# Scores computed twice in a fused attention and feed-forward kernel: once for the row maxima, once with the keys on partitions

## What is computed

```python
def _L0_xattn_ref(query, key, value, attn_mask, q_w, q_b, k_w, k_b, v_w, v_b, o_w, o_b):
    Q = proj(query, q_w, q_b)
    K = proj(key, k_w, k_b)
    V = proj(value, v_w, v_b)
    scores = jnp.einsum('bhqd,bhkd->bhqk', Q, K) / jnp.sqrt(jnp.float32(hd))
    scores = jnp.where(attn_mask, jnp.float32(-1000000000.0), scores)
    attn = jax.nn.softmax(scores, axis=-1)
    ctx = jnp.einsum('bhqk,bhkd->bhqd', attn, V)
    ctx = ctx.transpose(0, 2, 1, 3).reshape(B, S, D)
    out = jnp.einsum('bsd,ed->bse', ctx, o_w) + o_b
    return out
...
x = x + jnp.tanh(g_xattn[0]) * _L0_xattn_ref(_layernorm(x, axis=-1), ctx_1024, ctx_1024, ...)
x = x + jnp.tanh(g_ffn[0]) * _L0_ffn_ref(_layernorm(x, axis=-1), ...)
```

## Time and profile before

| | |
|---|---|
| runs | 1276.35 us median (1274.07, 1276.35, 1281.88) |
| span of the profiled execution | 1275.5 us, from first to last instruction; its own time is not listed beside it, and the span lies within the runs |
| TensorE matmul | 1184.9 us busy, 93% of the span, 7424 instructions |
| VectorE | 956.5 us, 75% |
| ScalarE | 763.2 us, 60% |
| GpSimd | 253.7 us, 20% |
| mean granted clock of TensorE | 0.977 of full |
| chain that ended last | TensorE 65%, VectorE 12%, issue 12%, GpSimd 6% |

### The profile page before, as it was taken

How to read it: one execution, slowest core, us unless ns; L and a number is a source line. 1 busy time by engine, 2 the same in 40 slices (tenths; PEclk the granted TensorE clock), 3 DMA queues, 4 the chain that set the end, 5 groups by cost and what they waited for, 6 DMA issues and landing times.

```text
span 1275.5 us, 25860 instructions
## 1 busy us (share of the span) xinstructions
PE 1184.9 (93%) x7424; PEld 933.5 (73%) x7424; DVE 956.5 (75%) x2011; ACT 763.2 (60%) x1632; POOL 253.7 (20%) x427
## 2 busy tenths in 40 slices
PE   3999899999999989999999999987999999999997
PEld 3777676777767767777676777765878878878886
DVE  5778688688778867868877887879677677777763
ACT  4678677678768867867866886774432433343332
POOL 1030030030012003003002100025433443343441
PEclk9999999999999989999998999987999999999999
DMA  6433332253243343233224332461111211211200
GB/s 216 113 96 80 100 108 61 70 143 79 64 125 89 79 98 91 76 99 106 75 59 134 82 83 59 115 196 52 51 50 64 84 49 49 99 49 49 78 37 34
DMA packets 72685, 109.81 MB, mean 86 GB/s; under 512 B 14864, under 2 KB 23696, under 8 KB 72592
## 3 DMA queue, kind: packets, MB, share of 16 engines
q1 hardware_dynamic: 72592, 108.92, 29.9%
HBM read 41.76 MB, written 16.78 MB: 46 GB/s over the span
## 4 chain that ended last, share of the span: by engine, by line
PE 65%; DVE 12%; issue 12%; POOL 6%; ACT 1%; POOLq 1%; DMA 1%; DVEq 1%; SPq 1%; ACTq 0%
PE bank L525 15%; PE bank L461 14%; PE bank L492 11%; PE bank L537 9%; PE bank L518 8%; PE bank L501 6%; DVE xh L992 3%; POOL newton L1094 2%; DVE neg_s L875 2%; PE bank L507 1%; POOL var_eps L1088 1%; DVE stats L832 1%; DVE pT L881 1%; DVE stats L981 1%; POOL rstd L1095 1%
## 5 line engine op out<-in xcount | busy, mean ns | idle before, releaser
L697 ACT ACTIVATE probs<-neg_s,negmax 128x512 f32<-128x512 f32 x512 | 368.3, 721 | 58.6 <-DVE negmax L875 50.5
L875 DVE CUSTOM_DVE_ANT_0 neg_s<-bank,mask_big 128x512 f32<-128x512 f32 x512 | 346.4, 684 | 63.7 <-PE bank L518 36.0
L525 PE MATMUL bank<-ident,probs 128*128 128x128 f32 x2048 | 320.7, 280 | 21.8 <-ACT probs L697 21.3
L525 PEld LDWEIGHTS bank<-ident,probs 128*128 128x128 f32 x2048 | 245.0, 143 | 82.5 <-ACT probs L697 43.0
L518 PE MATMUL bank<-k_stack,q_stack 96*128 96x512 f32 x512 | 247.8, 484 | 15.3 <-DVE negmax L875 15.3
L881 DVE COPY pT<-bank 128x512 f32<-128x512 f32 x256 | 176.5, 690 | 105.8 <-PE bank L525 104.6
L704 ACT COPY pT<-bank 128x512 f32<-128x512 f32 x256 | 149.2, 583 | 107.9 <-PE bank L525 104.1
L1088 POOL TENSOR_SCALAR var_eps<-mv 128x2 f32<-128x2 f32 (+1 forms) x24 | 16.6, 690 | 661.7 <-DVE mv L839 597.5
L537 PE MATMUL bank<-pT,v_sb 128*32 128x512 f32 x1024 | 118.8, 605 | 0.8 <-issue 0.5
L518 PEld LDWEIGHTS bank<-k_stack,q_stack 96*128 96x128 f32 x512 | 99.5, 195 | 22.3 <-DVE negmax L875 10.8
L697 ACT ACTIVATION_READ_ACCUMULATOR probs<-neg_s,negmax 128x1 f32 x512 | 97.0, 190 | 0.0
(11 more groups left out here) (111 smaller groups left out, 2169.5 us busy)
## 6 DMA issues: line engine op xcount, KB each, us to landing
k_stack<-k_hi SPq DMA_DIRECT2D x256, 64.0 KB, 2.0
q_stack<-q_hi SPq DMA_DIRECT2D x256, 64.0 KB, 2.0
x_rows<-x SPq DMA_DIRECT2D x8, 1024.0 KB, 6.9
cT_raw<-ctxT SPq DMA_DIRECT2D x8, 1024.0 KB, 5.5
k_stack<-k_lo SPq DMA_DIRECT2D x128, 64.0 KB, 2.0
q_stack<-q_lo SPq DMA_DIRECT2D x128, 64.0 KB, 2.0
ctx_dram<-ctx_sb SPq DMA_DIRECT2D x32, 256.0 KB, 2.1
c_raw<-ctx_dram SPq DMA_DIRECT2D x16, 512.0 KB, 4.2
```

The lines of the kernel that those rows point to most:

```text
L525: mm = nc.tensor.transpose(pt_bank[i % 2][:, a * P:(a + 1) * P], probs[:, i % P_RING, a * P:(a + 1) * P], ident[:])
L697: nc.scalar.activation(probs[:, i % P_RING, :], neg_s[:, i % SM_RING, :], ACT.Exp, bias=negmax[:, k:k + 1], scale=-1.0, accum_out=den[:, g ...
L875: nc.vector.tensor_tensor_reduce(neg_s[:, i % SM_RING, :], s_bank[i % S_BANKS][:], mask_big[:, q, :], 1.0, 3e38, ALU.add, ALU.min, negmax[ ...
```

## The change

The scores are computed twice. `max_scores` computes them as before, for the row minimum alone (`row_min`; the masked tile that it also writes is not used). The minimum of four tiles is split in two parts (`shift_parts`), turned by TensorE (`shift`), copied out by ScalarE (`shift_out`) and stored by SyncE as two more rows of `q_stack` (`shift_row`), against rows of -1 in `k_stack`. `scores` then computes the tile with keys on partitions from 98 rows, after a matmul of an identity by the transposed mask, into the same bank. `exp` writes the result straight to `pT`. GpSimd adds the four key tiles of each head (`key_sums`), a matmul of ones sums over the partitions (`denominator`), and the sums go through DRAM for their reciprocals. The context is stored undivided, and `normalise_context` divides it in stage two, on GpSimd but for the first batch. Q and K go through DRAM (`store_qk`, `stack_half`), six copies for each half of a group's heads, from one buffer for both in place of one each. The maxima run twelve tiles ahead of the scores. The inverse root of stage one moves from GpSimd to VectorE. The o projections of both units of the first batch stand in the last two groups of stage one. A slot is the sixteen steps of one group, each with one tile of scores, one maximum and a part of the side work from the table `SIDE`.

The tables of side work, first line of each:

```diff
-PE_SIDE = [
-    parts("K", 1, 0, 1, 3, 4) | parts("V", 2, 6, 7, 8, 9, 10, 11) | parts("Q", 2, 12, 13, 14, 16),
...
+SIDE = [
+    parts("Q", 2, 0, 2, 3, 4) + parts("K", 2, 6, 7, 8, 9) + parts("V", 2, 10, 11, 12, 13, 14, 15),
```

SyncE:

```diff
+            def store_qk(b, kind, n):
+                sp.wait_ge(side_done, done(side_no(b, (kind, n))))
+                apart(sp)
+                for part, t in enumerate((qk_hi, qk_lo)):
+                    sp.dma_start(qk_dram[n % 2, "QK".index(kind), part], t[:].bitcast(F32)).then_inc(qk_st, 16)
...
+            def shift_row(b, c, j):
+                sp.wait_ge(aux_out, shift_aux(b, c, j) + 1)
+                apart(sp)
+                sp.dma_start(stack[c % 2][0][BAND:CON, j, :].rearrange("r (q t) -> r q t", q=TT).bitcast(F32),
+                             shift_rows[:, j % 2, :].bitcast(F32)).then_inc(shifted[j], 16)
...
+            def slot(b, c):
...
+                    if not is_first(b, c):
+                        sp.wait_ge(s_mm, tile_no(b, c, 0))
                         apart(sp)
-                        load_x(b + 1)
...
+                    stack_half(b, c + 1, 1)
+                shift_row(b, c, 2)
+                if not is_first(b, c):
+                    store_context(*before(b, c))
+                    spread_den(*before(b, c))
+                shift_row(b, c, 3)
+                if c == 0 and not last:
+                    sp.wait_ge(side_mm, (side_no(None, ("T", TT - 1)) if is_first(b, c)
+                                         else side_no(b - 1, ("T", TT - 1))) + 1)
+                    apart(sp)
+                    load_x(b + 1)
+                    sp.wait_ge(c_done, b * CH + CH)
+                    apart(sp)
+                    load_ctx(b + 1)
+                if ahead and c != 1:
+                    store_qk(b, "Q", c + 2)
+                if not (last and c == 3):
+                    shift_row(b, c + 1, 0)
+                if ahead and c != 2:
+                    store_qk(b, "K", c + 2)
```

TensorE:

```diff
+            def max_scores(b, c, i):
+                j, q = i // TT, i % TT
+                if i % (TILES // 2) == 0:
+                    pe.wait_ge(stacked[c % 2][j // HALF], stack_count(b, c))
+                pe.wait_ge(max_min, tile_no(b, c, i) + 1)
+                q_stack, k_stack = stack[c % 2]
+                nc.tensor.matmul(max_bank[i % RING][:], q_stack[0:BAND, j, q * P:(q + 1) * P], k_stack[0:BAND, j, :],
+                                 start=True, stop=True).then_inc(max_mm, 1)
+            def shift(b, c, j):
+                pe.wait_ge(shift_lo, group(b, c) * GH + j + 1)
+                pe.wait_ge(aux_out, shift_aux(b, c, j))
+                nc.tensor.transpose(aux_bank[0:2 * TT, 0:P], nmin_parts[:].rearrange("p r q -> p (r q)").bitcast(F32),
+                                    ident[:]).then_inc(aux_mm, shift_events(b, c, j))
             def scores(b, c, i):
-                slot, j, q = where(c, i)
-                if i % TT == 0:
-                    for copied in stacked:
-                        pe.wait_ge(copied[j], (b * GROUPS + c + i // TILES + 1) * STACK_DMAS * 16)
-                pe.wait_ge(s_min, tile_no(b, c, i) + 1)
-                nc.tensor.matmul(s_bank[i % S_BANKS][:], stack[slot][0][:, j, q * P:(q + 1) * P],
-                                 stack[slot][1][:, j, :], start=True, stop=True).then_inc(s_mm, 1)
-            def transpose_probs(b, c, i):
-                pe.wait_ge(p_exp, tile_no(b, c, i) + 1 + SM_RING)
-                pe.wait_ge(pt_out[i % 2], b * (GROUPS * TILES // 2) + (c * TILES + i) // 2 + HEAD)
-                for a in range(TT):
-                    mm = nc.tensor.transpose(pt_bank[i % 2][:, a * P:(a + 1) * P],
-                                             probs[:, i % P_RING, a * P:(a + 1) * P], ident[:])
-                mm.then_inc(p_tr, 1)
+                j, a = i // TT, i % TT
+                q_stack, k_stack = stack[c % 2]
+                if a == 0:
+                    pe.wait_ge(shifted[j], group(b, c) * 16 + 16 + DMA_HEAD)
+                pe.wait_ge(p_exp, tile_no(b, c, i) + 1)
+                nc.tensor.matmul(s_bank[i % RING][:], ident_bf[:], maskT_big[:, a, :], start=True, stop=False)
+                nc.tensor.matmul(s_bank[i % RING][:], k_stack[:, j, a * P:(a + 1) * P], q_stack[:, j, :],
+                                 start=False, stop=True).then_inc(s_mm, 1)
...
+            def denominator(b, c):
+                pe.wait_ge(acc_done, group(b, c + 1) * GH + GH)
+                pe.wait_ge(aux_out, aux_no(b, c + 1, 0))
+                for j in range(GH):
+                    mm = nc.tensor.matmul(aux_bank[j * HD:(j + 1) * HD, :], ones[:], acc[:, j, :], start=True, stop=True)
+                mm.then_inc(aux_mm, 1)
...
+            def slot(b, c):
+                for i in range(TILES):
+                    scores(b, c, i)
+                    if i == EXTRA - 1 and not is_first(b, c):
+                        context(*before(b, c))
+                        denominator(*before(b, c))
+                    if next_max(b, c, i):
+                        max_scores(b, *next_max(b, c, i))
+                    for item in side_parts(b, c, i):
                         side(b, *item)
```

ScalarE:

```diff
             def exp(b, c, i):
-                if i == TILES:
-                    act.wait_ge(rden_ready, b * GROUPS + c + HEAD)
-                act.wait_ge(s_min, tile_no(b, c, i) + 1 + S_BANKS)
-                act.wait_ge(p_tr, tile_no(b, c, i) + 1)
-                g = (c + i // TILES) % 2
-                k = i % TILES
-                nc.scalar.activation(probs[:, i % P_RING, :], neg_s[:, i % SM_RING, :], ACT.Exp,
-                                     bias=negmax[:, k:k + 1], scale=-1.0,
-                                     accum_out=den[:, g, k:k + 1]).then_inc(p_exp, 1)
+                if i == EXTRA:
+                    act.wait_ge(pv_mm, group(b, c) + HEAD)
+                if i == EXTRA or i % TT == 0 and i:
+                    act.wait_ge(acc_done, group(b, c) * GH + i // TT + 1)
+                act.wait_ge(s_mm, tile_no(b, c, i) + 1)
+                nc.scalar.activation(prob_tile(c, i), s_bank[i % RING][:], ACT.Exp, scale=-1.0).then_inc(p_exp, 1)
             def context_hi(b, h):
-                act.wait_ge(c2_ld[h], b * 16 + 16)
-                if isinstance(b, int) and b + h == 0:
-                    for copied in (*stacked[0], *stacked[1]):
-                        act.wait_ge(copied, B * GROUPS * STACK_DMAS * 16)
+                act.wait_ge(c2_norm, b * 2 + h + 1)
```

VectorE:

```diff
-            def mean_and_variance(b):
+            def mean_and_rstd(b):
...
+                apart(dve)
+                inverse_root(dve, nc.vector, b * CHAIN, rstd_chain, mv[:, :, 1], var_eps[:], rstd[:], newton[:])
...
-            def mask_and_min(b, c, i):
-                _, _, q = where(c, i)
-                k = i % TILES
-                dve.wait_ge(s_mm, tile_no(b, c, i) + 1 + HEAD)
-                dve.wait_ge(p_exp, tile_no(b, c, i) + 1)
+            def row_min(b, c, i):
+                q = i % TT
+                dve.wait_ge(max_mm, tile_no(b, c, i) + 1)
                 apart(dve)
-                nc.vector.tensor_tensor_reduce(neg_s[:, i % SM_RING, :], s_bank[i % S_BANKS][:], mask_big[:, q, :], 1.0,
-                                               3e38, ALU.add, ALU.min, negmax[:, k:k + 1]).then_inc(s_min, 1)
...
+                nc.vector.tensor_copy(nmin_parts[:, 0, :], nmin[:, cols]).then_inc(shift_hi, 1)
+                dve.wait_ge(shift_hi, k + 1)
+                nc.vector.tensor_tensor(nmin_parts[:, 1, :], nmin[:, cols], nmin_parts[:, 0, :],
+                                        ALU.subtract).then_inc(shift_lo, 1)
...
+            def slot(b, c):
+                last = is_last(b)
+                for i in range(TILES):
+                    if next_max(b, c, i):
+                        row_min(b, *next_max(b, c, i))
+                    for at, item in side_outs(b, c, i):
+                        side(at, *item)
+                    if c == 0 and not last and 8 <= i < 8 + TT:
+                        row_stats(b + 1, i - 8)
+                    if c == 0 and not last and i == 13:
+                        mean_and_rstd(b + 1)
+                    if c == 1 and not last and i >= TILES - CH:
+                        context_in(b, i - TILES + CH)
+                    if i == 10 and not is_first(b, c):
+                        reciprocal(*before(b, c))
```

GpSimd:

```diff
+            def key_sums(b, c, j):
+                link = (group(b, c) * GH + j) * (TT - 1)
+                pool.wait_ge(aux_mm, aux_no(b, c, 0) + 1)
+                for a in range(1, TT):
+                    pool.wait_ge(p_exp, tile_no(b, c, j * TT + a) + 1 + RING)
+                    if a > 1:
+                        pool.wait_ge(acc_chain, link + a - 1)
+                    first = prob_tile(c, j * TT) if a == 1 else acc[:, j, :]
                     apart(pool)
...
```

(8 more changed lines are left out.)

889 lines of the change are left out of this document (482 added, 407 removed).

## The result

The changed kernel takes **1507.8 us** (median of 4 runs, 1503.5 to 1509.9) against 1277.4 for the kernel before in the same comparison: a ratio of 1.179, 95% interval 1.176 to 1.183. The forecast was 1384, with a range to 1480: slower, as forecast, but by 230 us and not by 108, and beyond the end of the range.

The account below looks back on a forecast made before the run. It took TensorE's order of work to bound the first stage and a loop over VectorE, GpSimd and ScalarE the second. 1275.5 + 77 to the first k matmul + 28 second stage + 3 first unit = 1384 us, range 1300 to 1480.

Parts of the forecast that it names:

- rival (d): TensorE's three matmuls of a step hide no weight load: 0.31 us each, 0.225 a tile more, 1499 us; chance 0.05.
- (a): Loads come early enough or TensorE's lead carries the slots: a batch's waits 1 us, not 17; 1241 us; chance 0.10.
- (c): GpSimd becomes the bound: an addition of 512 costs 2.08 us, 11 more a batch; 1461 us; chance 0.07.
- (b): First-stage root on VectorE blocked by a GpSimd addition at each link: 18 us, not 3.7; 1482 us; chance 0.08.
- the forecast's 11 us: Slot 0 of a batch ends 11 us late, through waits for x load, Q store and root: 36 in place of 24.7.
- the forecast's 17: Waits a batch: 11 us in slot 0, 4 in slot 1, 2 for small waits; bounds 9 and 26.
- The forecast's own bounds: Whole kernel: waits of 9 to 26 us a batch, plus the second stage's bounds, gave 1311 to 1457 us.
- That is inside the 11, as VectorE sets the pace meanwhile: Slot 0: idle TensorE falls to 0.50 of its clock, at no cost beyond the 11 us of lateness.
- the sum had 100: TensorE's work in a first-stage batch, summed from instruction prices: 100 us, 7 more than before.
- the whole port effect: Slot 1: VectorE and GpSimd block each other at their shared port, 2 us added, bounds none and 7.
- the last batch, "98": Last batch to the first k matmul: 24.7 + 24.7 + 23 + 19.5 + 4.5 and 2 of waits, 98 us.
- The queue argument: Slot 0: SyncE's small copies behind the x and context loads cannot pass them; statistics wait 4 us, K output 6.

Follow-up runs that it names:

- experiment 6: Changed kernel with GpSimd making one of the three additions of a denominator and VectorE's reciprocal of the sums made a copy: 1454.4 us.
- The repaired kernel: Changed kernel with early loads, root links between minima, split last-batch loads, remainder before root, division first, K before Q: 1386.6 us, 1.084 to the kernel before.
- experiment 3: Changed kernel with the next batch's x and context loads issued from ScalarE's queue, at the same point of slot 0: 1491.5 us.

## Why the prediction was too low

**Held.** A tile on TensorE costs 0.69 (0.705 forecast), which ends rival (d), whose 1499 lies near the measured time by chance. The load is issued at 14.7 (14), the statistics are late by 3.4 (4), ScalarE by 5.5 (6). Additions take 1.3 (1.22). The unit is 26.8 (26.6), nearly all of the growth through the division. Of the rivals, (a) and (c) did not happen; (b) priced fifteen blocked links, and in the batch shown two were blocked.

**Held by luck.** TensorE's three waits in slot 0 add up to the forecast's 11 us, but the root was priced at 3 us and took 6.5: a link is 0.31 from start to start and not 0.2, and two links were blocked. The forecast's 11 was also the whole lateness of the slot, which is 14.7 (39.4 against 24.7). Slot 1 takes 28.8 us (28.7 forecast), but with 1.3 us of idle time and 1.8 of lower clock where the forecast had 4 of waits. The batch's idle time of 16.8 us is the forecast's 17, but as 11.0, 1.3, 3.6 and 0.9 by slot, not as 11 and 4 and 2 for all small waits. The forecast's own bounds, redone from its terms, are 1300 to 1459 and not 1311 to 1457; 1508 lies outside both.

**Failed: the clock after a wait.** "That is inside the 11, as VectorE sets the pace meanwhile" is the step that failed in slot 0. The stretch at 1.2 GHz comes after the wait, when TensorE sets the pace, and costs 4.9 us more a batch; with the 1.7 of slot 2 it is 6.6, most of the 9 us by which the batch is longer than forecast. The rest is work: 109.3 us busy less 6.6 is 102.7, where the sum had 100. The earlier trace rows gave 0.50 in a wait; the 4 us behind it, in which the clock stays at 0.50 and TensorE is busy all the time (466 to 470), should have been read too.

**Failed: slot 2, taken as a slot with small waits.** It was set at 26.1, with no more than the 2 us for small waits on top, and is 32.2: TensorE waits 3.1 us for x remainders, and 3.8 us at a clock of 0.55 follow. VectorE is late there with context remainders of 1.3 and 1.8 us, slowed by additions. The forecast put the whole port effect into slot 1; experiment 6 found it mostly in slots 0 and 2. The two steps together are the batch at 126 in place of 117, 65 us to the end of the seventh batch.

**Failed: the last batch, "98".** Largest for its length: it takes 139.5 us to the first k matmul, 41 more than forecast, with TensorE idle for 33 of them and a mean clock of 0.85. It was summed from TensorE's work with 2 us for waits. It was not asked what SyncE issues there (5 MB ahead of shift rows that TensorE now needs), nor what stands behind the first unit's root on VectorE. The queue argument had been made for slot 0 and stopped there.

**Smaller.** The first slot begins at 61.0 and not 53, since Q was ready for storing 6 us later than taken. Most of these 6 us are on VectorE: its four normalisations of the first x take 6.96 us in all (from 19.15) beside a GpSimd instruction of 5.68 on the transposed mask (from 19.70), where the earlier trace rows had 0.54 each. The end of the program is 10 us longer than forecast: the first unit lost 13.8 and not 5, with the weight splits now inside it and VectorE and GpSimd side by side; no run separates the two. 8 + 65 + 41 + 10 = 124, which is 1508 less 1384.

**What these repairs do not give back.** The repaired kernel is 108.5 us of span behind the one before: 35 until the first context, 56 to the last batch, 11 in it, 6 behind it. By the windows shown above, the 56 are 32 us of TensorE's busy time, at almost the same clock, and 24 of waits (53 against 29 idle). So the added work is 4.6 us a batch, where the forecast gave TensorE 7 (93 to 100), and nearly half of what is left is still waits. Slots 1, 2 and 3 have 1.3, 2.6 and 0.9 us of idle time a batch, against 0, 1.2 and 0 before; slot 0 has about as much as before (3.2 to 3.9 against 3.3 to 3.6).

## What to carry to other kernels

Where a kernel gains a short transfer that its bottleneck engine waits for, list every large transfer of the same queue in every stage, the transitions above all, and not only at the place first looked at. A serial chain of tiny operations delays everything behind it in its engine's order by its whole length, however little work it is (6.5 us here for 2.5 of work): put it on an engine with no one waiting, and expect each link to lose up to one long instruction of the port's other user. Behind waits of some us, add the stretch in which TensorE works at half its clock, and take its length from rows of such places, past the wait and not only in it: it is not the length of the wait alone that decides (see below).

## What the runs showed of the chip that was not expected

Waits of 4.4 and 4.8 us on TensorE are followed by 3.2 and 6.6 us at 1.2 GHz, while the waits themselves are recorded at 1.00. A wait of 2.2 us in slot 2, with one of 0.9 us some 5 us ahead of it, is followed by such a stretch too (about 3.7 us, from 269.0), and one of 3.1 us in slot 0 of experiment 3 (up to 207.3) is not: the clock stays at 1.00 there. A copy of four elements a partition on VectorE takes 0.84 us at the median beside GpSimd's additions of 1.29, and 0.17 when two of three of them are left out. A matmul's record can include the one ahead of it in the same accumulation: 616 ns in the record, 0.45 us from start to start for both.
